# Writing the running sums of a state-space mixer to memory: two stores in place of four, and the layout of the two intermediate tensors

## Time and profile before

| | before |
|---|---|
| median of 3 runs | 1644.7 us (1642.37 to 1646.21) |
| the profiled execution: own time, span | 1645.84 us, 1644.0 us |
| mean granted TensorE clock | 0.998 of full |
| TensorE busy | 1621.2 us, 99% of the span |
| VectorE busy | 1034.7 us, 63% |
| ScalarE busy | 626.3 us, 38% |
| GpSimd busy | 378.9 us, 23% |
| DMA, mean | 290.46 MB, 177 GB/s |
| stores of `aS` | 16 of 128 KB each |
| loads of `mvg` and `stn` | 64 of 32 KB each |

### The profile page before, as it was taken

The page is one execution under the profiler, slowest core; times in us unless marked ns, Lnnn a source line. Parts: engine busy times, 40 slices in busy tenths (PEclk is TensorE's granted clock), DMA queues, the critical chain, the costliest instruction groups (busy, mean ns, idle before and its releaser), DMA issues.

```text
span 1644.0 us, 25044 instructions
## 1 busy us (share of the span) xinstructions
PE 1621.2 (99%) x9672; PEld 1313.0 (80%) x9672; DVE 1034.7 (63%) x2022; ACT 626.3 (38%) x934; POOL 378.9 (23%) x298
## 2 busy tenths in 40 slices
PE   6999999999999999999999999999999999999999
PEld 3788888878888778888787888877888878888887
DVE  6543445785677877777776768777775684543333
ACT  5333343464333463333454334355333341122111
POOL 1666652012212212122122122122122121000000
PEclk9999999999999999999999999999999999999999
DMA  9745654754444444454445444445444437556763
GB/s 325 275 172 212 231 192 172 263 183 149 164 163 160 144 156 150 151 169 157 143 162 162 158 152 159 157 131 194 156 156 157 156 127 224 167 181 191 215 203 129
DMA packets 252403, 290.46 MB, mean 177 GB/s; under 512 B 14464, under 2 KB 211200, under 8 KB 243072
## 3 DMA queue, kind: packets, MB, share of 16 engines
q1 hardware_dynamic: 252288, 288.88, 53.0%
HBM read 238.51 MB, written 50.33 MB: 176 GB/s over the span
## 4 chain that ended last, share of the span: by engine, by line
PE 74%; DVE 3%; ACT 1%; issue 1%; DMA 0%; SPq 0%; ACTq 0%; DVEq 0%
PE bank L1191 31%; PE bank L1232 14%; PE bank L1147 12%; PE bank L1260 5%; PE bank L1329 3%; PE bank L1300 2%; PE bank L1316 2%; PE bank L1278 2%; PE bank L1288 1%; PE bank L1323 1%; DVE xT L1750 0%; DVE res L1776 0%; DVE m_cv L1792 0%; DVE m_L L1823 0%; DMA cum_stay<-m_aS 0%
## 5 line engine op out<-in xcount | busy, mean ns | idle before, releaser
L1191 PE MATMUL bank<-fxT,wj 128*128 128x512 f32 x1752 | 415.2, 390 | 0.0
L1191 PEld LDWEIGHTS bank<-fxT,wj 128*128 128x128 f32 x1752 | 328.7, 188 | 68.5
L1232 PE MATMUL bank<-m_wd,m_hb 128*128 128x512 f32 x1128 | 278.8, 393 | 0.0
L1232 PEld LDWEIGHTS bank<-m_wd,m_hb 128*128 128x128 f32 x1128 | 209.2, 188 | 44.9 <-issue 2.4
L1544 ACT CAST m_hb<-xn 128x512 fp32r<-128x512 f32 x96 | 59.5, 620 | 452.5 <-DVE xn L1763 452.5
L1147 PE MATMUL bank<-xT,wi 128*128 128x512 f32 x900 | 224.4, 397 | 1.6 <-DVE m_cv L1792 0.5
L1147 PEld LDWEIGHTS bank<-xT,wi 128*128 128x128 f32 x900 | 167.2, 189 | 40.1 <-issue 5.1
L1776 DVE TENSOR_TENSOR res<-bank,res 128x512 f32<-128x512 f32 x192 | 132.5, 690 | 83.0 <-PE bank L1232 80.9
L2099 POOL TENSOR_TENSOR m_L<-m_L,m_GT 128x512 f32<-128x512 f32 x36 | 52.8, 1466 | 434.4 <-ACT m_L L1553 434.4
L1763 DVE SCALAR_TENSOR_TENSOR xn<-bank,sc,xn 128x512 f32<-128x512 f32 x96 | 71.7, 747 | 121.6 <-PE bank L1191 121.5
L1538 ACT ACTIVATE xn<-bank,sc 128x512 f32<-128x512 f32 x96 | 66.1, 689 | 146.3 <-PE bank L1191 140.9
(11 more groups left out here) (224 smaller groups left out, 2317.8 us busy)
## 6 DMA issues: line engine op xcount, KB each, us to landing
wj<-ug_split SPq DMA_DIRECT2D x167, 512.0 KB, 4.2
m_wd<-dn_split SPq DMA_DIRECT2D x48, 1024.0 KB, 4.8
wi<-in_split SPq DMA_DIRECT2D x76, 512.0 KB, 3.2
ug_split<-b_wu SPq DMA_DIRECT2D x8, 2048.0 KB, 14.0
m_wo<-out_split SPq DMA_DIRECT2D x32, 512.0 KB, 4.1
wi<-ug_split SPq DMA_DIRECT2D x25, 512.0 KB, 4.2
in_split<-b_msp SPq DMA_DIRECT2D x20, 512.0 KB, 3.8
raw<-in_wug SPq DMA_DIRECT2D x8, 1024.0 KB, 6.8
```

The costliest lines, as they stand in the source:

```text
L1191: ins = pe.matmul(to[:], w[:, a, k, :], frm[:, b, k, :], start=(k == 0 and i == 0), stop=(k == KH - 1 and i == 2))
L1232: ins = pe.matmul(F[t % 2][:], hb[:, a, j, ck(t)], wd[:, b, j, :], start=(j == 0 and n == 0), stop=(j == 1 and n == 2))
```

## The change

The two parts of `aS` go out in one store per form, two stores in all in place of four: first `cum_stay`, then `cum_move`. For that, `cum_move` is laid out [2 parts, 8 blocks, 8 heads, 512] and `cum_stay` [8 chunks, 2 parts, 64 heads, 64], so that in each store the 128 partitions step evenly through memory. The count that SyncE waits for falls from 64 to 32 per item. The loads read the same bytes: that of `mvg` now takes its 16 rows as two pieces of 8 rows, 128 KB apart, where they lay in one piece; that of `stn` reads its 16 rows in the order chunk, part where it was part, chunk. The rows of `mvg` that pick chunks are written in that order too, by the same instruction with other slices.

```diff
-    cum_m = nc.dram_tensor("cum_move", [NB, 2 * HPB, SEQ], F32, kind="Internal").ap()
-    cum_s = nc.dram_tensor("cum_stay", [2, SEQ // 64, HEADS, 64], F32, kind="Internal").ap()
+    cum_m = nc.dram_tensor("cum_move", [2, NB, HPB, SEQ], F32, kind="Internal").ap()
+    cum_s = nc.dram_tensor("cum_stay", [SEQ // 64, 2, HEADS, 64], F32, kind="Internal").ap()
...
             def keep(q):
 
                 sp.wait_ge(s_as, q + 1)
-                for l in range(2):
-                    src = aS[HEADS * l:HEADS * (l + 1), :].bitcast(F32)
-                    sp.dma_start(cum_m[:, HPB * l:HPB * (l + 1), :], src).then_inc(s_kp, 16)
-                    sp.dma_start(cum_s[l].rearrange("k h s -> h k s"), src.rearrange("h (k s) -> h k s", k=NK)).then_inc(s_kp, 16)
+                src = aS[:].bitcast(F32)
+                sp.dma_start(cum_s.rearrange("k l h s -> (l h) k s"), src.rearrange("p (k s) -> p k s", k=NK)).then_inc(s_kp, 16)
+                sp.dma_start(cum_m.rearrange("l b h s -> (l b h) s"), src).then_inc(s_kp, 16)
                 if q == 0:
                     load_in(5)
-                sp.wait_ge(s_kp, 64 * q + 64)
+                sp.wait_ge(s_kp, 32 * q + 32)
 
             def heads(q, b):
 
                 wait(sp, s_A, QUADS * (NB * q + b))
-                sp.dma_start(mvg[0:2 * HPB, :].bitcast(F32), cum_m[b]).then_inc(s_ld, 16)
+                sp.dma_start(mvg[0:2 * HPB, :].bitcast(F32), cum_m[:, b]).then_inc(s_ld, 16)
                 sp.dma_start(stn[2 * HPB:ROWS].rearrange("r j s -> r (j s)").bitcast(F32),
-                             cum_s[:, :, HPB * b:HPB * (b + 1), :].rearrange("l k h s -> (l k) (h s)")).then_inc(s_ld, 16)
+                             cum_s[:, :, HPB * b:HPB * (b + 1), :].rearrange("k l h s -> (k l) (h s)")).then_inc(s_ld, 16)
...
+            pairs = unit(2 * HPB, 2 * NK).rearrange("p (k l) -> p k l", l=2)
             dve.scalar_tensor_tensor(mvg[0:ROWS].rearrange("p (k l) -> p k l", k=NK),
-                                     unit(2 * HPB, NK).unsqueeze(2).to_broadcast([ROWS, NK, QL]), -1.0,
-                                     unit(2 * HPB + NK, NK).unsqueeze(2).to_broadcast([ROWS, NK, QL]),
+                                     pairs[:, :, 0:1].to_broadcast([ROWS, NK, QL]), -1.0,
+                                     pairs[:, :, 1:2].to_broadcast([ROWS, NK, QL]),
                                      ALU.mult, ALU.subtract).then_inc(s_z0, 1)
```

## The result

The changed kernel takes 1649.78 us (median of 10 runs, 1647.48 to 1652.71) against 1643.25 us for the kernel before in the same comparison (10 runs, 1642.37 to 1646.21). The ratio is 1.0037, 95% interval 1.0027 to 1.0047: slower, by about 6 us, where 1.2 us less was forecast. (The forecast started from 1644.7 us, the median of three runs, which lies 1.4 us above the median of ten.) The profiled execution took 1648.98 us.

The account below looks back on a forecast made before the run. TensorE was taken as the bound; gains of 1.0 us (item 3), 0.19 (item 1), 0.05 (item 2) and 0 (item 0) sum to 1.24 us, giving 1643.5 us from the median 1644.7, range 1641.0 to 1646.8.

Parts of the forecast that it names:

- The bound and the place: TensorE, busy 1621.2 of 1644.0 us, sets the time; store and load waits reach it before each item's first decay product.
- the loads of blocks 1 to 7: Later loads in each item: issued 9.9 us before use at the tightest, at least 5.2 us of cover.
- The load of `mvg` in two pieces: Read of 16 rows before the decay product: taken as no change, since rows and their size stay the same.
- The bound of 1.57 us: Upper bound for the `mvg` load: fifteen more rows one after another if it became a single stream.
- The rule of the Trainium skill: For the `mvg` read: two engines with eight rows each, 0.73 us more, 0.2 us past `stn`; gain about 1.0 us.
- The issue of the stores, 1.0 us earlier: SyncE's queue: two of four store issues per item go, landing 1.0 us earlier; item 3 gains 1.0 of 1.26 us.
- The lower bound: For the stores' landing: no gain, if DMA traffic sets the landing and hides the issues; upper bound 1.33 us.
- Item 0, covered by VectorE: First item's decay product: gain 0 because VectorE's backlog sets its end; without that cover up to 0.82 us.
- The slow read as a rival: Block 0 of each item: `mvg` load in one stream lands 1.57 us later; 5.1 us slower, 1649.8 us; chance 0.06.

Follow-up runs that it names:

- Experiment 8: Kernel before plus a 512-byte gap in `cum_move`; block 0 of each item loads `mvg` as two whole 8-row loads, blocks 1 to 7 in two pieces; ratio 0.9998.
- experiment 1: Kernel before with only a 512-byte gap between the halves of each block's rows in `cum_move`, so the `mvg` load takes two pieces; ratio 1.0032, 1649.79 us.
- experiment 3: Changed kernel with the `mvg` rows ordered head, part, so its load begins with a dimension of 8, not 2; ratio 1.0015 to the kernel before.
- experiment 2: Kernel before with only the store into `cum_stay` merged; `cum_move` keeps its layout and two stores; ratio 1.0004.
- experiment 4: Changed kernel with the `mvg` load issued as two loads of 8 rows, one per part; ratio 1.0012 to the kernel before, 1645.37 us.
- experiment 9: No `cum_move`: `mvg` loaded straight from tile `aS`, two 8-row loads per block, only the `cum_stay` store left; ratio 1.0000 to the kernel before, 1644.38 us.

## Why the prediction was wrong

**The bound and the place: right.** TensorE is the bound, the stores and loads of the running sums reach it only at the first decay product of each item, and the loads of blocks 1 to 7 are covered. Experiment 8 shows it within its interval. The spare time of those loads was read a little too long: one of item 0's is used 9.3 us after its issue, not 9.9.

**The load of `mvg` in two pieces: the step that failed.** The prediction took no change, "since the rows it writes and their size are the same". The runs showed 0.96 us more per item on average, two streams in place of sixteen, and this alone makes the loss (experiments 1 and 8). The bound of 1.57 us held it. The rule of the Trainium skill that stood beside the step gave the two streams, and it was left out of the sum; the packet counts bear it out. But the price put on it there, 0.73 us for eight rows in a line less 0.5 to spare, 0.2 net, was too low as well, for two reasons. SyncE's issue of such a pattern takes 0.67 to 0.75 us on this path, not 0.33, and holds up the load of `stn` behind it: 0.38 us (experiment 3). This term wasn't in the prediction at all. The rows themselves were priced high enough (0.104 us each, 0.08 in the packets). What was missing is the pause of about 0.5 us in the two streams, behind which nearly all of the load and two rows of `stn` stand. The load part scatters from 2.65 to 3.5 us with it. Why it comes isn't shown.

**The issue of the stores, 1.0 us earlier: wrong.** The last store does go out about 1.6 us sooner after the first (0.4 us behind it, not 2.0), but the store part is 6.76 us on average against 6.69. The lower bound, nothing, was the right one. Merged in one form or in both, the stores land no sooner (mean 6.54 in experiment 2, 6.72 in experiment 4; over all profiles, the five with two stores have a mean of 6.81 and the five with four stores 6.78). Item 3's 7.43 us, from which the gain was taken, was simply the longest of four; the other three were already 6.1 to 6.9. So the place to gain was itself largely chance.

**Item 0, covered by VectorE: half right.** An earlier load gives nothing there (experiment 9). But a later one costs its full 0.83 us: from the start of the transposes to `from_states` it is 11.09 us before (356.58 to 367.67) and 11.92 after (355.65 to 367.57), with the same wait of 0.65 us at its end. The cover was judged by the first exponential (358.90 against 359.71, 0.81 us), while the two that follow had 0.40 and 0.03 us to spare. The slack of a chain is that of its tightest link, and a stretch at balance gives nothing one way and takes everything the other.

**Item by item**, the sum that should have stood there: 0.83 + 1.96 + 1.26 + 0.09 = 4.1 us, from the profile after. This is the sum of one execution; at an equal clock the runs say about 4.7, and with the clock 5.7. The 1.96 of item 1 is the slow load (0.99) on top of a store part that happened to take 0.96 us longer, and item 3's 0.09 is the slow load less a store part that was 0.86 shorter; over many runs the scatter evens out and the load stays.

**The slow read as a rival** had the place and the sign, at 0.06. It was given a delay that decides at 1.5 us, because the stores were to give 1.0 back, and two streams were called short of it. Without that gain, and with the issue counted, it decides at once. That its price of 5.1 us was near the 5.7 measured, and its time of 1649.8 us next to the median, is luck: it was made of one stream in place of two, 0.25 us for item 0 in place of 0.83, and a second fall of the clock (1.7 us) that neither profile of the changed kernel shows.

**What would have shown it beforehand:**. Sixteen completions per load said that a load is cut into streams, and the step from 16x512 to 2x8x512 was the one thing in the change that could alter how.

## What to carry to other kernels

Before changing the layout of a tensor in memory, write down the outermost dimension of every transfer that touches it, on both sides, and keep the ones on the critical path at sixteen: merging two stores that are hidden by traffic isn't worth a read that has to be waited for. Count a transfer's cost in issue time on its queue as well as in landing time, because the next load stands behind it. A wait of a tenth of a per cent on the bound engine can hardly be won and easily be doubled, so look first at what a change could cost there.

## What the runs showed of the hardware

A load of 16 rows of 2 KB runs in 16, 8 or 2 streams, shown by its completions (512, 256 and 64 for 32 loads), and from its issue to its first use, with a second load behind it, takes 2.3, 2.7 and 2.65 to 3.5 us (mean 3.1 of 24). Where two streams were late (3.2 to 3.3 us in the changed kernel), they paused for about 0.5 us, with a row of 0.54 to 0.62 us where most took 0.08; where they didn't (experiment 1, three items), the load took as long as with eight. The issue itself took 0.33 us on an idle path for a pattern with one step and 0.66 to 0.80 us for one with two. With one store of 1024 pieces of 256 bytes the stores landed as late as with two of 512 each (6.54 against 6.69 us to the load behind them). Over all runs the changed kernel's 4.1 and 5.4 us of longer waits came with 5.7 us of time and a mean granted clock 0.0007 to 0.0008 lower.
